# Four indirect scatters spread between GpSimd's other operations in a fused attention and expert kernel

## The reference

```python
def reference(x, ctx_1024, Wq, bq, ..., router_w, router_b, weights1, bias1, weights2, bias2):
    # cross attention, 128 batches of 128 tokens, width 256, 16 heads of 16
    q, k, v = layernorm(x) @ Wq.T + bq, ctx_1024 @ Wk.T + bk, ctx_1024 @ Wv.T + bv
    x = x + softmax(q k.T / 4) v @ Wo.T + bo
    # each token goes to one of 32 experts (argmax of the router)
    h = layernorm(x)
    e = argmax(h @ router_w.T + router_b)
    return x + relu(relu(h @ weights1[e] + bias1[e]) @ weights2[e] + bias2[e])
```

## Time and profile before

| what | value |
|---|---|
| time, median of 3 runs | 1454.6 us (1454.57 to 1455.21) |
| the profiled execution | 1464.87 us, its span 1463.1 us |
| TensorE busy | 1250.0 us, 85% |
| VectorE busy | 1020.0 us, 70% |
| ScalarE busy | 783.1 us, 54% |
| GpSimd busy | 667.6 us, 46% |
| the four scatters of a block (L360) | 128, 129.0 us busy, 1008 ns each |
| add_bo (L324) | 32, 75.8 us busy, 2368 ns each |
| granted TensorE clock, mean | 0.951 |

### The profile page before, as it was taken

One profiled execution on the slowest core, in us unless ns is written; L12 is line 12 of the kernel. 1 busy time (PEld: TensorE's weight loads), 2 busy tenths in 40 slices (PEclk: granted clock), 3 DMA queues, 4 the chain that ended last, 5 costly groups with the idle time before them and its releaser, 6 DMA issues. The chain is left out here.

```text
span 1463.1 us, 43093 instructions
## 1 busy us (share of the span) xinstructions
PE 1250.0 (85%) x15172; PEld 892.3 (61%) x15173; DVE 1020.0 (70%) x2867; ACT 783.1 (54%) x1602; POOL 667.6 (46%) x811
## 2 busy tenths in 40 slices
PE   4999999899989998999899899999973388777776
PEld 3666666666656665666666666666652266656654
DVE  3678888878878887888688878888876244433342
ACT  3566666656656665666466656666644133333332
POOL 4344444434444553454344434454424155545554
PEclk9999999989999999999999999999986599999998
DMA  2611221111111111212121111111100655566542
GB/s 96 220 45 60 65 98 61 61 60 60 60 61 60 60 67 53 67 67 86 36 93 68 60 60 60 60 60 60 45 17 34 168 172 173 181 175 178 153 134 67
DMA packets 87297, 126.60 MB, mean 87 GB/s; under 512 B 11521, under 2 KB 69132, under 8 KB 87054
## 3 DMA queue, kind: packets, MB, share of 16 engines
q1 hardware_dynamic: 67678, 68.97, 16.5%
q0 software_dynamic: 19440, 55.15, 10.2%
HBM read 68.95 MB, written 59.31 MB: 88 GB/s over the span
## 5 line engine op out<-in xcount | busy, mean ns | idle before, releaser
L587 DVE TENSOR_REDUCE mx<-scores 128x8 bf16<-128x1024 f32 x256 | 307.7, 1222 | 40.6 <-PE scores L814 38.4
L466 ACT ACTIVATE pv<-scores 128x1024 f32<-128x1024 f32 x256 | 248.2, 1021 | 79.9 <-PE scores L836 79.9
L392 POOL DMA_INDIRECT out<-work x160 | 157.9, 987 | 163.6 <-DVE work L752 115.3
L458 ACT ACTIVATE mxT<-b 128x128 bf16<-128x128 f32 x128 | 35.5, 277 | 306.4 <-PE b L821 306.4
L360 POOL DMA_INDIRECT pages<-row,slot_i x128 | 129.0, 1008 | 80.1 <-issue 53.6
L855 PE MATMUL b<-wo_s,work 128*128 128x256 f32 x512 | 148.4, 413 | 19.1 <-DVE work L604 19.1
L846 PE MATMUL b<-pv 128*32 128x128 f32 x4096 | 143.3, 279 | 14.0 <-issue 10.5
L829 PE MATMUL scores<-qM,kT 32*128 32x256 f32 x2048 | 152.2, 410 | 0.1
L1008 PE MATMUL scores<-pv,zt 128*128 x320 | 116.9, 450 | 35.0 <-issue 14.7
L752 DVE SCALAR_TENSOR_TENSOR work<-scores,work 128x256 f32<-128x256 f32 x160 | 67.6, 422 | 101.6 <-PE scores L1008 61.1
L544 ACT ACTIVATE row<-b 128x256 f32<-128x256 f32 x160 | 61.0, 381 | 141.4 <-PE b L991 97.0
(11 more groups left out here) (121 smaller groups left out, 2556.3 us busy)
## 6 DMA issues: line engine op xcount, KB each, us to landing
work<-pages SPq DMA_DIRECT2D x40, 520.0 KB
xs<-x_in SPq DMA_DIRECT2D x32, 512.0 KB, 5.9
work<-ctxT SPq DMA_DIRECT2D x32, 512.0 KB, 7.2
pages<-empty POOLq DMA_DIRECT2D x30, 520.0 KB, 6.3
row<-w SPq DMA_DIRECT2D x160, 64.5 KB
pages<-empty POOLq DMA_DIRECT2D x1, 5200.0 KB, 23.2
out<-work POOLq DMA_INDIRECT x160
pv<-w SPq DMA_DIRECT2D x1, 2080.0 KB
```

The costliest lines, as they stand in the source:

```text
L392: pool.indirect_dma_start(out_rows, bass.IndirectOffsetOnAxis(pr[:, r, COL_TOKEN:COL_TOKEN + 1].bitcast(U32), 0), pr[:, r, 0:D], None, bou ...
L466: act.activation(pt[:, u % 2, 2 * p:2 * p + 2], scores4[:, 1024 * p:1024 * (p + 1)].rearrange("p (j k) -> p j k", j=2), ACT.Exp).then_inc( ...
L587: dve.tensor_reduce(mx[:, u % 2, 8 * p:8 * (p + 1)], scores4[:, 1024 * p:1024 * (p + 1)].rearrange("p (h k) -> p h k", h=8), AX.X, ALU.max ...
```

## The change

`scatter` issues one of the four transfers, the one of batch u, and is called four times in a step, each time with its waits. Between the calls stand the operations that followed the four: add_bo between the first and the second, rstd1 between the second and the third, fill_more between the third and the fourth. rstd1 and fill_more have changed places.

```diff
-            def scatter(q, r4, at):
+            def scatter(q, r4, u, at):
                 apart(pool, ("slot_out", q + 1), ("fill", q * 16 + 16 if at < NQ - 1 else 16 * (NQ - 1)))
-                for u in range(QB):
-                    pool.indirect_dma_start(
-                        pages, bass.IndirectOffsetOnAxis(slot_i[:, r4, u:u + 1], 0), row[:, r4, u, :], None,
-                        bounds_check=last_slot, oob_is_err=False).then_inc(S[f"scattered{r4}"], 16)
+                pool.indirect_dma_start(
+                    pages, bass.IndirectOffsetOnAxis(slot_i[:, r4, u:u + 1], 0), row[:, r4, u, :], None,
+                    bounds_check=last_slot, oob_is_err=False).then_inc(S[f"scattered{r4}"], 16)
...
                 if has(at, -3):
-                    scatter(s - 3, (k - 3) % NR, at - 3)
+                    scatter(s - 3, (k - 3) % NR, 0, at - 3)
                 if has(at, 1):
                     add_bo(s + 1, 1 - par, at + 1)
+                if has(at, -3):
+                    scatter(s - 3, (k - 3) % NR, 1, at - 3)
+                if has(at, 2):
+                    rstd1(s + 2, at + 2)
+                if has(at, -3):
+                    scatter(s - 3, (k - 3) % NR, 2, at - 3)
                 if has(at, 2):
                     fill_more(s)
-                    rstd1(s + 2, at + 2)
+                if has(at, -3):
+                    scatter(s - 3, (k - 3) % NR, 3, at - 3)
```

## The result

The changed kernel takes 1505.27 us (median of 4 runs, 1501.13 to 1505.83) against 1454.59 for the kernel before in the same comparison. The ratio is 1.034, interval 1.031 to 1.037: slower by 50.7 us. The forecast of slower was right; its 1485 us is 20 us short. The profiled execution has a span of 1503.0 us.

What follows compares the result with a forecast made beforehand. TensorE was taken as the bound, without slack over most of a step. Per step 2.15 − 1.07 = 1.08 us; 28 of these plus 0.3 give 30.5, so 1454.6 becomes 1485 us; range for 8 in 10 1478 to 1516.

Steps and rivals of the forecast that it cites:

- case A: The forecast itself, in the steps with scatters and add_bo: stall outweighs the lifted hold, 1481 to 1491 us; chance 0.63.
- rival B: At the spread scatters: VectorE's stall comes and TensorE's signals stay held or move, up to 1515 us; chance 0.17.
- add_bo stops VectorE: Behind scatter 0: add_bo blocks VectorE's small operations, delaying the residual L612 by 2.15 us a step (2.04 to 2.31).
- Rival C: At add_bo's new place: it doesn't catch L641, VectorE isn't stopped, only the gain is left, 1425 us; chance 0.16.
- The hold goes (−1.07): Before VectorE's L593 of batch 1: the late TensorE signal's wait disappears, gaining 1.07 us a step.
- Scattered alone, signals go: At the spread scatters: lone scatters don't hold TensorE's signals, scatters in a row do; gain 1.07 us a step.
- The single scatter of the earlier trace: Expert stage, scatter at 1210.84: ScalarE's L544 had only an ordinary 0.92 us wait, taken to show single scatters hold nothing.
- TensorE is full from there on: After L855, the first output projection: TensorE has no slack, so the step stays 1.08 us longer (0.97 to 1.24).
- The sum: Over 28 steps at 1.08 us each, plus 0.3 for the tail: 30.5 us slower (27 to 35).
- carrying the steps of a profiled execution over to the median of the runs: Whole kernel: the change computed for the profiled 1464.87 us is added whole to the runs' median, 1454.6, giving 1485.
- The 0.3 us for the tail: At the stage's end, last block's scatters: three more groups of waits cost 0 to 0.3 us each, 0.3 in all.
- Edits costed at nothing: On GpSimd in the step: rstd1 ahead of the fill and the fill some 6 us later were both said to cost nothing.

Runs made afterwards that it cites:

- Experiments 1: Changed kernel with add_bo and scatter 1 in exchanged places, so add_bo follows two scatters: 1432.6 us, ratio 0.986 to the kernel before.
- 2: Kernel before with only add_bo moved, to between scatters 0 and 1; fill and rstd1 last as before: 1515.1 us, ratio 1.044.
- 3: Changed kernel with add_bo adding the bias for batch u = 0 only (all batches in the first block): 1452.2 us, ratio 0.999 to the kernel before.
- experiment 12: Changed kernel reordered to scatters 0 and 1, add_bo, scatter 2, rstd1, scatter 3, fill: 1441.3 us, ratio 0.986 to the kernel before.
- experiment 11: Changed kernel reordered to scatters 0 and 1, add_bo, fill, rstd1, scatters 2 and 3: 1471.5 us, ratio 1.007 to the kernel before.
- experiment 5: Kernel before with only rstd1 and the fill in changed places, four scatters still in a row: 1363.8 us against 1362.9, ratio 1.000.
- 10: Third-set repeat of the changed kernel with add_bo and scatter 1 in exchanged places: 1440.6 us, ratio 0.9855 to the kernel before.
- run 9: The changed kernel once more without an edit, in the third set: 1517.2 us, ratio 1.038 to the kernel before.
- experiment 6: Changed kernel with add_bo as four instructions of 128x256 in place of one of 128x1024: 1450.6 us, ratio 1.062 to the kernel before.

## Why it was right, and where the size was off

The direction and its cause were right. The measured 1505 us lies outside the 1481 to 1491 of case A and inside the part of the range that was there for rival B.

**add_bo stops VectorE (2.15 us a step): right, mis-sized.** It measures 2.46 us (3.86 − 1.40), 0.31 more. The prediction let the collision begin at L638 or L641. It is the cast L634, due 0.27 us ahead of add_bo's start, that is caught. The four small operations between it and the residual then come behind add_bo, not ahead of it. The prediction read that very cast's stall in the earlier trace rows, but counted only operations that start at add_bo's start or behind it. Experiments 1, 2 and 3 show the mechanism: away with add_bo's place or with its length. Rival C, that VectorE slips through, is out. Why a cast that starts 0.24 us ahead of the long add_bo is caught, and the same cast ahead of the short one isn't, stays open. The Trainium skill, "SBUF — State Buffer", section "Who interferes with whom", gives the ports to whichever was issued first. By the starts in the trace it doesn't agree: the cast starts at 640.85, add_bo at 641.09, and the cast is the one that stands. What the records call a start may lie ahead of the moment at which the ports are asked for; no run shows that.

**The hold goes (−1.07): right, a little more.** The step where nothing is held is 1.18 us shorter (32.55 − 31.37), and all of it goes at this place: behind the residual the transpose stands 3.37 us in the changed kernel, 4.53 before.

**"Scattered alone, signals go": the step that failed.** Rival B had it, in part: scatter 2, with the fill 1.11 us behind it, holds the attended values of the next quarter (due at 654.19, seen at 654.86). The third output projection shows 7.78 us from the second in place of 7.27 (24.76 − 16.98, 21.78 − 14.51): +0.5 us a step that the sum didn't have. The single scatter of the earlier trace rows was read rightly, and 22 more in its stage agree (experiment 12). It didn't carry over to the first stage, and why stays open. The fill behind scatter 2, which B named and the sum gave no cost, is a candidate. Where signals are held, only experiment 11 took it away from the late scatters, and those are a pair.

**"TensorE is full from there on" was not all.** In 17 of the 28 steps the first projection stands 9.60 to 9.73 us behind the scatter, not 9.2. The last section shows why. It adds little here, since a later TensorE meets less of the hold behind scatter 2: in those steps the third projection comes 7.36 to 7.50 us behind the second, and the step is 34.4 either way. So 11 of the 28 steps lose their last half microsecond to the hold, and 17 to TensorE's clock.

**The sum.** Per step +2.46 − 1.18 + 0.51 = 1.79 of the 1.85 us by which plain steps got longer (34.40 − 32.55), where 1.08 was forecast. 28 × 1.85 = 52 us; 50.7 were measured. That this fits so well is in part luck. In the two traces the 28 steps differ by 46.2 us (993.8 against 947.6), since not all of them are plain, and the spans by 39.9, since the expert stage is shorter in the second (289.3 against 293.9). So carrying the steps of a profiled execution over to the median of the runs was sound to some 10 us, not better. The 0.3 us for the tail can't be seen beside that.

**Edits costed at nothing** (rstd1 ahead of the fill, fill later, rows and pages): right in experiment 5, where no signal is held. For the sets with held signals only 10 and 12 bear on it: with the fill ahead of the last scatter or behind it the time is the same (1440.6 and 1441.3 us).

Not settled: what holds the signals, and why one set of runs is free of it.

## What to carry to other kernels

Before an operation of one engine moves, lay its whole duration over the other engine's timeline at the new place. Take in the small operation that starts just ahead of it, and count all that is queued behind the one caught: 1.3 us of placement moved this kernel by 5% (1432.6 against 1505.3). Cutting the operation into pieces doesn't help while they stand back to back. A wait that goes from one place is only gone when every later signal near the moved transfers has been looked at, for all readers, ScalarE too.

## What was not expected of the hardware

**Held signals come and go with the circumstances of the run.** The same kernel before took 1454.5 and 1462.4 us in two sets and 1362.9 in one (17 runs, 1359.4 to 1366.3). The second and the third set were run on the same numbered chip, so it doesn't go with the chip's number. About a third of the 92 to 100 us is the first stage (28 × 1.18 = 33 us). The rest is the expert stage: from its first scatter to its last it takes 293.9 us before (1163.4 to 1457.3) and 229.7 in experiment 5 (1127.5 to 1357.2), with the same 160 scatters of the same 0.97 us. Held signals are there too: of ScalarE's waits for L991 (now L997) 41 end over 0.1 us behind the matmul in the kernel before, 66 us in all, and none in experiment 5. That these 66 us are the 64 is not shown; not all of them need be on the chain that sets the time.

**A pause of TensorE of 2.4 us can cost its clock behind it.** Busy time by stretch in run 9 (stretch, length, PE, PEld, DVE, ACT, POOL, clock, transfers):

```profile
644.00:648.00 4.00, 2.58 (x20) 1.06 (x20) 3.86 (x14) 3.21 (x5) 3.35 (x2) 1.00 0.11 37
648.00:650.50 2.50, 1.56 (x36) 1.36 (x37) 2.36 (x9) 0.00 (x0) 1.18 (x2) 0.99 0.43 35
650.50:655.00 4.50, 4.50 (x47) 3.52 (x46) 4.40 (x11) 1.13 (x3) 0.00 (x0) 0.62 0.66 245
655.00:676.00 21.00, 20.87 (x303) 14.82 (x301) 17.45 (x42) 14.01 (x28) 9.91 (x17) 1.00 0.12 40
```

TensorE idles 2.36 us before its L852 at 648.94, works for 1.56 us again, and the granted clock is 0.62 from 650.50 to 655.00, so much of that stretch at 1.2 in place of 2.4 GHz. The first projection is 0.44 us later than in steps where the clock stays at 1.00. The changed kernel's first profile shows a clock below 0.9 at this place in 17 of 28 steps, run 9 in 14, and experiment 6, whose pause is 2.5 us, in 25. Experiments 1 and 10, whose pauses there are some 0.6 us, show it in none. In the kernel before, whose pauses are 0.5 and 0.64 us, it is 2 of 28, both more than 0.5 us later at this place (one of them shows 0.60 from 589 to 593 us). So a long pause makes it frequent, but a short one doesn't rule it out.
